# The expert work of a token mixer and router cut into five groups of chunks in place of four

## The chip, the core and the metric

One core of a Trainium2 chip runs the whole kernel. The metric is the device time in microseconds: 777.89 us is the median of three runs of the kernel before (777.68 to 777.95). The five engines are called PE (TensorE, with PEld for its weight loads), DVE (VectorE), ACT (ScalarE), POOL (GpSimd) and SP (SyncE, which issues most DMAs).

## The reference

```
h = tok(x)                  # four shifted copies + layer norm + 8x8 patch convolution: 16 images x 169 tokens x 128
h = concat([h, txt], 1)     # + 512 text tokens per batch item: 16 x 681 tokens, 128 wide
h = h + attn(layernorm(h))  # p_t * cumsum(p_s * x) @ mix_w.T + mix_b, along the tokens
h = h + ffn(layernorm(h))

# ffn: 8 experts, hidden width 256, the best 2 of 8 for each token
logits = xf @ Wg;  topw, topi = top_k(logits, 2);  topw = softmax(topw)
g, u = split(xf @ Wgu[e] + bgu[e]);  eo[e] = (silu(g) * u) @ Wd[e] + bd[e]
out  = sum over the two chosen experts of weight * eo
```

## The kernel before

The tokens are cut into 23 chunks of at most 4 x 128 tokens: 7 image chunks (4 x 104 tokens, the last one half as wide) and 16 text chunks, in the order 3 image, 4 text, 4 image, 12 text. Each chunk goes through attention, the second layer norm, the router (logits, the two best experts), and gets a place for each of its (token, expert) pairs. POOL then writes the chunk's normed rows to those places in the DRAM buffer `xbuf` with indirect DMAs, called scatters here (L1051, 8 for a chunk of width 4).

The chunks are gathered into groups (`GROUPS`, L67). When a group's last chunk has its places, the numbers of tokens of each expert are known and the group is closed: DVE makes a table of expert tiles (`tile_table`) and turns places in `xbuf` into places in `ybuf` (`places_of_results`), SP fills the gaps with zero rows (`pad`, 8 DMAs). From then on the group's expert tiles can run. A tile is 256 rows of one expert: SP loads its rows (L567) and its expert's weights (L570, 450 KB), PE turns the rows (`tile_T`, L791), multiplies by the gate and up weights (`gate_up`), ACT and DVE make silu(g) * u (L947, L1491), PE multiplies by the down weights (`down`), DVE adds the bias (`row_keep`, L1500) and SP stores 256 rows to `ybuf` (L576). After the group's last tile is stored, POOL fetches each token's two result rows with indirect DMAs, called gathers (L1065, 8 for a chunk of width 4); DVE weighs and adds them (`combine`, L1511 and L1515) and SP stores the chunk of the output (L583 for text, L589 for images).

How many tiles a group needs is fixed ahead of the data: `KT[g] = (2 * tokens + 8 * 255) // 256`, since each of 8 experts can leave a tile nearly empty. Likewise `xbuf` has room for the worst case, plus 8 spare tiles of zero rows for each group.

The order of the work on every engine is written by one clock of slots: iteration i has 16 slots, and slot number 16 * i + s says which step is issued. In iteration i chunk i is placed (slot 4) and scattered (slots 5 to 14), while later chunks stand at earlier steps (`AT`). A closed group's tiles begin at slot 6 of the iteration after its last chunk, and `spread` lays them evenly over the slots up to where the next group's tiles begin; the last group has 2 slots per tile. The gathers of a group are spread in the same way, from 6 slots behind its last tile to where the next group's tiles end. Engines wait for each other by semaphores, so a slot has no fixed length; all engines pass the slots in this order, and a late step holds back what is queued behind it on its engine. In the first iterations the second half of the images is worked in as well.

```
TILE_FROM = [b * SLOTS + 6 for a, b in GROUPS]
TILE_TO = TILE_FROM[1:] + [TILE_FROM[-1] + 2 * KT[-1]]
GATHER_FROM = [b + GATHER_LAG for b in TILE_TO]           # 6 slots
GATHER_TO = TILE_TO[1:] + [TILE_TO[-1] + GATHER_LAG + 16]
```

Of the kernel before, what the change touches and what calls it, by code (L numbers as in the profile page):

```python
# [63 lines left out]
SLOT = 256  # L64
SUB = SLOT // P
SHIFT = 8
GROUPS = [(0, 4), (4, 12), (12, 19), (19, 23)]  # L67


def width(n):  # L70
# [7 lines left out]
def cols_of(n):  # L78
    return parts(n) * width(n)


def group_of(n):
    return next(g for g, (a, b) in enumerate(GROUPS) if a <= n < b)


NTOK = [sum(cols_of(n) for n in range(a, b)) for a, b in GROUPS]
CAP = [(-(-n // SLOT) + 1) * SLOT for n in NTOK]
KT = [(2 * n + E * (SLOT - 1)) // SLOT for n in NTOK]
ROW0 = [sum(E * CAP[j] + E * SLOT for j in range(g)) for g in range(len(GROUPS) + 1)]
TILE0 = [sum(KT[:g]) for g in range(len(GROUPS) + 1)]  # L90
TILES = TILE0[-1]
KMAX = max(KT)

QUAD = 4
GROUP_POS = max(b - a for a, b in GROUPS) * W4 * 2


def tile_group(k):
    return next(g for g in range(len(GROUPS)) if k < TILE0[g + 1])

# [1525 lines left out]
```

## Time and profile before

| | |
|---|---|
| median of the runs | 777.89 us |
| the profiled execution | 779.29 us, its span 777.5 us |
| PE matmul busy | 579.0 us (74%) |
| PE weight load busy | 510.3 us (66%) |
| POOL busy | 474.0 us (61%) |
| DVE busy | 463.0 us (60%) |
| ACT busy | 235.7 us (30%) |
| mean granted TensorE clock | 0.815 of full speed |

The share of each engine is a mean over stages that differ. A stage can be found by the placing of a chunk, the DVE instruction of L1366: chunk 0 is placed at 93.56 us, chunk 3 at 147.38, chunk 11 at 307.07, chunk 18 at 472.93 and the last one, chunk 22, at 606.51. PE's last tile ends near 725 us, and the rest is POOL's gathers with DVE and SP behind them.

### The profile page before, as it was taken

To read this page: it belongs to the slowest core of one execution; us is meant where nothing else is said; L and a number is where in the kernel's file an instruction comes from. 1 tells how busy PE (TensorE), PEld (TensorE's weight loads), DVE (VectorE), ACT (ScalarE), POOL (GpSimd) and SP (SyncE) were. 2 spreads that over 40 slices of the span, in tenths; PEclk is the share of its full clock that TensorE was granted. 3 is DMA by queue.
4 is the path that set the end of the run, shared out by engine and by line. 5 is a ranking of instruction groups with operands and counts; after the bars stand their busy time and mean duration, and the time that the engine had idled before them with its cause. 6 is when DMAs were issued, how large, how long until landed. Compare 5 with 4: busy or idle time off the path is not lost. (4 is left out here: it accounts for less than half of the span.)

```text
span 777.5 us, 12251 instructions
## 1 busy us (share of the span) xinstructions
PE 579.0 (74%) x3221; PEld 510.3 (66%) x3221; DVE 463.0 (60%) x1838; ACT 235.7 (30%) x576; POOL 474.0 (61%) x504
## 2 busy tenths in 40 slices
PE   3793558666896986799998988889798788988200
PEld 2692447654775775688787877779687676887100
DVE  4667787765546567747767666736565553565322
ACT  3511412210423233234344441434433232433000
POOL 5513377734757564547776775637777772777674
PEclk9997556765968688769989896979999989999755
DMA  7298000204446353367776665569878787999322
GB/s 151 58 319 204 14 24 26 84 15 165 124 144 169 114 174 107 109 204 225 209 220 200 181 211 179 154 215 274 248 214 248 253 239 222 292 315 296 100 81 61
DMA packets 85130, 132.93 MB, mean 171 GB/s; under 512 B 14818, under 2 KB 58330, under 8 KB 85062
## 3 DMA queue, kind: packets, MB, share of 16 engines
q1 hardware_dynamic: 73062, 109.39, 46.9%
q0 software_dynamic: 11520, 22.35, 9.4%
q10 hardware_dynamic: 480, 0.41, 0.4%
q8 instruction: 27, 0.44, 0.2%
q14 instruction: 41, 0.34, 0.1%
HBM read 92.01 MB, written 43.75 MB: 175 GB/s over the span
## 5 line engine op out<-in xcount | busy, mean ns | idle before, releaser
L619 PE MATMUL gu<-space,wts 128*128 128x256 f32 x912 | 252.8, 419 | 1.8 <-DVE space L1491 1.8
L1051 POOL DMA_INDIRECT xbuf<-x,pos x180 | 185.0, 1028 | 68.5 <-issue 59.2
L1065 POOL DMA_INDIRECT gat<-ybuf,ypos x180 | 176.7, 982 | 72.3 <-issue 56.9
L1491 DVE SCALAR_TENSOR_TENSOR space<-gu,wts,space 128x256 f32<-128x256 f32 x228 | 108.4, 481 | 186.3 <-ACT space L947 113.5
L947 ACT ACTIVATE space<-gu,wts 128x256 f32<-128x256 f32 x228 | 107.2, 472 | 318.3 <-PE gu L619 311.5
L619 PEld LDWEIGHTS gu<-space,wts 128*128 128x128 f32 x912 | 181.2, 213 | 24.5 <-DVE space L1491 2.6
L619 PEld LDWEIGHTS dn<-wts,space 128*128 128x128 f32 x912 | 128.4, 206 | 34.5 <-DVE space L1491 28.2
L619 PE MATMUL dn<-wts,space 128*128 128x128 f32 x912 | 132.4, 292 | 20.8 <-DVE space L1491 20.0
L993 POOL TENSOR_TENSOR rs<-ve,nhalf 128x4 f32<-128x4 f32 (+2 forms) x39 | 41.3, 1058 | 74.0 <-DVE ve L1288 43.3
L791 PE MATMUL xTp<-cst,space 128*128 128x128 f32 x228 | 51.1, 310 | 20.3 <-DMA space<-xbuf 20.2
L1500 DVE TENSOR_TENSOR space<-dn,wts 128x256 f32<-128x256 f32 x114 | 47.3, 415 | 3.8 <-PE dn L619 3.7
L791 PEld LDWEIGHTS xTp<-cst,space 128*128 128x128 f32 x228 | 30.5, 159 | 28.2 <-DMA space<-xbuf 24.0
L941 ACT COPY space<-xTp 128x256 f32<-128x256 f32 x114 | 41.4, 363 | 23.0 <-PE xTp L791 23.0
L619 PE MATMUL mx<-mixT,yT 128*128 128x128 f32 x128 | 34.3, 430 | 14.3 <-DVE rank L1366 8.5
L1511 DVE SCALAR_TENSOR_TENSOR gat<-gat,w,space 128x128 f32<-128x128 f32 x64 | 18.2, 346 | 44.6 <-DMA gat<-ybuf,ypos 44.6
L619 PEld LDWEIGHTS mx<-mixT,yT 128*128 128x128 f32 x128 | 31.1, 327 | 16.2 <-issue 16.1
L619 PEld LDWEIGHTS tr<-wg,x2T 128*128 128x128 f32 (+1 forms) x180 | 32.3, 263 | 4.8 <-issue 2.9
L929 ACT ACTIVATE x<-space,sh,rs 128x128 f32<-128x128 f32 x64 | 26.3, 486 | 25.7 <-POOL sh L1035 25.7
L619 PE MATMUL dn<-wtokT,space 128*104 128x128 f32 x260 | 34.0, 296 | 0.0
L619 PEld LDWEIGHTS dn<-wtokT,space 128*104 128x104 f32 x260 | 33.4, 192 | 0.0
L1041 POOL TENSOR_TENSOR ex<-euler,gap 128x4 f32<-128x4 f32 (+2 forms) x23 | 23.6, 1026 | 12.5 <-DVE gap L1314 12.0
L619 PE MATMUL tr<-wg,x2T 128*128 128x8 f32 (+1 forms) x180 | 30.9, 300 | 0.0
(190 smaller groups left out, 690.2 us busy)
## 6 DMA issues: line engine op xcount, KB each, us to landing
wts<-wall SPq DMA_DIRECT2D x114, 450.0 KB, 4.5
space<-xbuf SPq DMA_DIRECT2D x114, 128.0 KB
ybuf<-space SPq DMA_DIRECT2D x114, 128.0 KB
xt<-in_txt_dram SPq DMA_DIRECT2D x16, 256.0 KB, 4.1
xbuf<-zero_rows SPq DMA_DIRECT2D x4, 1024.0 KB, 11.2
xbuf<-zero_rows SPq DMA_DIRECT2D x32, 128.0 KB
out_dram<-gat SPq DMA_DIRECT2D x16, 256.0 KB
xbuf<-x,pos POOLq DMA_INDIRECT x180
```

The costliest lines, as they stand in the source:

```text
L619: return nc.tensor.matmul(o, l, r, start=a, stop=z_)
L791: last = nc.tensor.transpose(xT_ps[:, s * P:(s + 1) * P], xrow[k % NX][:, s * D:(s + 1) * D], ident)
L929: last = nc.scalar.activation(x2[n % NX2][0:p, j * D:(j + 1) * D], h1_of(n)[0:p, j * D:(j + 1) * D], ACT.Identity, bias=sh2[0:p, j:j + 1], ...
L941: copy(xT[k % 2], xT_ps[:, 0:SLOT]).then_inc(W.xs_ok, 1)
L947: nc.scalar.activation(sil[q % 3], gu_ps[q % 3][:, 0:SLOT], ACT.Silu, bias=wts[k % NW][:, W_B + t:W_B + t + 1]).then_inc(W.sil_ok, 1)
L993: tt(out_[0:p, 0:w], var[0:p, 0:w], nhalf[0:p, 0:w], ALU.pow).then_inc(done, 1)
L1041: tt(ex[0:p, 0:w], euler[0:p, 0:w], gap[0:p, 0:w], ALU.pow).then_inc(W.ex_ok, 1)
L1051: nc.gpsimd.indirect_dma_start(out=xbuf, out_offset=bass.IndirectOffsetOnAxis(pos[0:p, c:c + 1], 0), in_=x2[n % NX2][0:p, m // 2 * D:(m // ...
L1065: nc.gpsimd.indirect_dma_start(out=gat[b][0:p, (k * W4 + j) * D:(k * W4 + j + 1) * D], out_offset=None, in_=ybuf[g], in_offset=bass.Indire ...
L1491: V.scalar_tensor_tensor(hid[q % 4], gu_ps[q % 3][:, SLOT:2 * SLOT], wts[k % NW][:, W_B + HT + t:W_B + HT + t + 1], sil[q % 3], ALU.add, A ...
L1500: V.tensor_tensor(yrow[k % NYB].rearrange("p (s d) -> p s d", s=SUB), dn_ps[k % 2][:, 0:SUB * D].rearrange("p (s d) -> p s d", s=SUB), wts ...
L1511: last = V.scalar_tensor_tensor(rows[1][j], rows[1][j], wn[1][j], h1_of(n)[0:p, j * D:(j + 1) * D], ALU.mult, ALU.add)
```

## The change

`GROUPS` has five groups that end at chunks 4, 10, 16, 20 and 23, in place of four that end at 4, 12, 19 and 23. Nothing else is edited; everything that hangs on the table follows.

```diff
-GROUPS = [(0, 4), (4, 12), (12, 19), (19, 23)]
+GROUPS = [(0, 4), (4, 10), (10, 16), (16, 20), (20, 23)]
```

What follows from it, by the kernel's own formulas:

| | before | after |
|---|---|---|
| tokens of each group | 1760, 3504, 3584, 2048 | 1760, 2784, 2768, 2048, 1536 |
| tiles of each group | 21, 35, 35, 23 (114) | 21, 29, 29, 23, 19 (121) |
| slots where the tiles begin | 70, 198, 310, 374 | 70, 166, 262, 326, 374 |
| slot where the last tiles end | 420 | 412 |
| gathers of each group | 32, 60, 56, 32 (180) | 32, 48, 44, 32, 24 (180) |
| slots of the gathers | 204 to 310, 316 to 374, 380 to 420, 426 to 442 | 172 to 262, 268 to 326, 332 to 374, 380 to 412, 418 to 434 |
| pad DMAs, spare DMAs of 1 MB | 32, 4 | 40, 5 |

PE's queue around the place of chunk 10, kernel before (mx<-mask are the ranks of a chunk, mx<-mixT the attention's product of a later one, gu and dn are tile work, x22 a buffer of normed rows):

```order
L744 MATMUL tr<-cst,x22 128x128 x4
L619 MATMUL mx<-mask,tri_r 104x16
L619 MATMUL mx<-mask,ones_r 104x8
L619 MATMUL mx<-seen0,ones_r 104x16
L619 MATMUL gu1<-space,wts0 128x256 x2
L619 MATMUL dn0<-wts4,space 128x128 x4
L619 MATMUL mx<-mixT,yT 128x128 x4
L619 MATMUL mx<-mixb2,ones_r 128x512
L619 MATMUL tr<-wg,x2T 128x8 x4
L791 MATMUL xTp<-cst,space 128x128 x2
L619 MATMUL gu2<-space,wts1 128x256 x2
```

The same place in the changed kernel:

```order
L744 MATMUL tr<-cst,x22 128x128 x4
L619 MATMUL gu2<-space,wts0 128x256 x2
L619 MATMUL dn1<-wts4,space 128x128 x4
L619 MATMUL dn0<-wts0,space 128x128 x4
L619 MATMUL mx<-mask,tri_r 104x16
L619 MATMUL mx<-mask,ones_r 104x8
L619 MATMUL mx<-mixT,yT 128x128 x4
L619 MATMUL mx<-mixb2,ones_r 128x512
L791 MATMUL xTp<-cst,space 128x128 x4
L619 MATMUL gu0<-space,wts1 128x256 x2
```

Chunk 10 now begins a group: its ranks no longer add what was counted before (the seen row is gone). The first group's tiles end here with two down products in a row, and the next group's begin with two turned tiles in a row; before, tile work ran across this place without a seam.

POOL's queue at its very end, kernel before (xbuf<- are scatters, gat<- gathers, ybuf1 to ybuf3 the result buffers of groups 1 to 3, counted from 0):

```order
L1051 DMA xbuf<-x21,pos 104448x128
L1065 DMA gat<-ybuf1,ypos 104x128
L1051 DMA xbuf<-x21,pos 104448x128
L1065 DMA gat<-ybuf1,ypos 128x128 x8
L1065 DMA gat<-ybuf2,ypos 128x128 x56
L1065 DMA gat<-ybuf3,ypos 128x128 x32
```

And in the changed kernel:

```order
L1051 DMA xbuf<-x21,pos 108544x128
L1065 DMA gat<-ybuf2,ypos 128x128
L1051 DMA xbuf<-x21,pos 108544x128
L1065 DMA gat<-ybuf2,ypos 128x128 x8
L1065 DMA gat<-ybuf3,ypos 128x128 x32
L1065 DMA gat<-ybuf4,ypos 128x128 x24
```

Behind the last scatter stand 8 + 32 + 24 gathers in place of 8 + 56 + 32, and the final block, which waits for the last tile, has 24 in place of 32.

## Rows read from the trace of the kernel before

**Rows 1.** The page: busy time of two engines, share of the span, instructions.

```profile
PE 579.0 (74%) x3221; PEld 510.3 (66%) x3221; DVE 463.0 (60%) x1838; ACT 235.7 (30%) x576; POOL 474.0 (61%) x504
```

**Rows 2.** Chain that ended last, from 722 us: start, us, what.

```profile
725.30 2.62 DMA ybuf<-space
...
729.46 0.95 POOL gat L1065
...
767.14 0.95 POOL gat L1065
```

**Rows 3.** Timeline of POOL: start, us, what, idle before and its releaser.

```profile
655.46 1.07 POOL L1065 DMA_INDIRECT gat<-ybuf,ypos  x1 [14.52 <-DMA ybuf<-space]
...
725.53 0.95 POOL L1065 DMA_INDIRECT gat<-ybuf,ypos  x1 [0.30 <-issue]
```

**Rows 4.** Stretches: length, PE, PEld, DVE, ACT, POOL busy (instructions), clock, DMA share, GB/s.

```profile
201.10:251.00 49.90, 38.90 (x221) 33.50 (x219) 26.28 (x144) 16.66 (x43) 32.44 (x36) 0.83 0.55 159
251.00:307.10 56.10, 45.32 (x223) 38.60 (x223) 34.56 (x160) 19.06 (x49) 30.34 (x36) 0.77 0.46 135
307.10:331.40 24.30, 17.99 (x83) 15.73 (x83) 17.85 (x80) 6.06 (x15) 11.63 (x13) 0.71 0.32 101
331.40:355.90 24.50, 23.09 (x114) 19.63 (x114) 13.93 (x61) 9.64 (x25) 14.03 (x16) 0.76 0.67 217
355.90:472.90 117.00, 108.31 (x601) 95.10 (x601) 79.35 (x340) 46.45 (x120) 84.76 (x90) 0.91 0.70 207
472.90:501.50 28.60, 24.95 (x125) 21.82 (x125) 19.74 (x84) 9.07 (x23) 17.37 (x18) 0.82 0.53 162
501.50:539.30 37.80, 33.93 (x185) 30.43 (x185) 19.41 (x72) 13.22 (x33) 19.51 (x21) 0.86 0.73 227
539.30:606.50 67.20, 59.14 (x353) 53.31 (x352) 37.67 (x144) 22.57 (x57) 51.15 (x53) 0.95 0.81 244
...
645.00:728.10 83.10, 70.18 (x419) 61.88 (x418) 44.53 (x126) 27.91 (x69) 53.80 (x56) 0.98 0.86 272
```

**Rows 5.** Stretches, tile turns of L791 alone, two for a tile: length, PE, PEld, clock.

```profile
251.00:307.10 56.10, 3.70 (x16) 2.32 (x16) 0.77 0.46 135
...
355.90:472.90 117.00, 10.87 (x50) 6.38 (x50) 0.91 0.70 207
...
539.30:606.50 67.20, 7.22 (x36) 4.57 (x36) 0.95 0.81 244
```

**Rows 6.** The page's costliest groups, PE matmuls of the tiles, 114 tiles.

```profile
L619 PE MATMUL gu<-space,wts 128*128 128x256 f32 x912 | 252.8, 419 | 1.8 <-DVE space L1491 1.8
...
L619 PE MATMUL dn<-wts,space 128*128 128x128 f32 x912 | 132.4, 292 | 20.8 <-DVE space L1491 20.0
...
L791 PE MATMUL xTp<-cst,space 128*128 128x128 f32 x228 | 51.1, 310 | 20.3 <-DMA space<-xbuf 20.2
```

**Rows 7.** Timeline of PE around 505 us, the first tiles of the third group.

```profile
505.16 0.44 PE L791 MATMUL xTp<-cst,space 128*128 128x128 f32 x2 [0.82 <-DMA space<-xbuf]
508.33 0.69 PE L791 MATMUL xTp<-cst,space 128*128 128x128 f32 x2 [2.73 <-DMA space<-xbuf]
```

**Rows 8.** Timeline of DVE, placing of chunks 16 and 17.

```profile
424.24 0.19 DVE L1366 TENSOR_TENSOR rank<-mx,off_f 128x32 f32<-128x32 f32 x1
...
448.60 0.18 DVE L1366 TENSOR_TENSOR rank<-mx,off_f 128x32 f32<-128x32 f32 x1
```

**Rows 9.** Chain that ended last, 660 to 700 us.

```profile
668.53 1.73 PE gu L619 x8
...
674.21 1.74 PE gu L619 x8
...
694.77 0.43 SPq L583
...
695.38 4.95 DMA space<-xbuf
```

**Rows 10.** Timeline of PE, a wait for a tile's rows in the last group.

```profile
700.37 0.44 PE L791 MATMUL xTp<-cst,space 128*128 128x128 f32 x2 [1.20 <-DMA space<-xbuf]
```

## The prediction

> **What bounds the kernel now.** I read the chain that ended last first, then POOL's timeline, then a table of stretches cut at the placing of chunks. The chain ends in one engine: after the last tile's results have landed (725.30 + 2.62 = 727.9 us) POOL issues 32 gathers, one each (767.14 - 729.46) / 30 = 1.256 us, and nothing overlaps them [rows 2]. The stretch before, 645.0 to 728.1 us, holds the 23 tiles of the last group. PE is busy for 70.2 of 83.1 us at clock 0.98, and POOL gathers there without a break from 655.46 to 726.5 us [rows 3, 4]: PE and POOL end within 2 us of each other, so both bound it.
>
> Farther back the reader is to see three densities [rows 4, 5]. From 251.0 to 307.1 us three chunks pass with 16 tile turns, which is 8 tiles: 18.7 us a chunk at 2.67 tiles, PE busy 81%, clock 0.77. From 355.9 to 472.9 us five chunks pass with 25 tiles: 23.4 us a chunk at 5, PE busy 93%, clock 0.91. From 539.3 to 606.5 us two chunks pass with 18 tiles: 33.6 us a chunk at 9, PE busy 88%, while POOL issues 53 instructions in 67.2 us, 1.27 us each, which is its full pace. So the kernel is near PE's limit from 331 us on, near POOL's as well from about 520 us, and has room only before 331 us. Over the whole span PE is busy 74% and POOL 61% [rows 1], which hides this.
>
> **The change part by part.** The work is moved as the table of slots shows: 7 more tiles in all, 4 fewer behind slot 374, hence 11 more before it.
>
> *Gathers behind the last tile.* 24 in place of 32: 8 x 1.256 = 10.0 us less [rows 2]. Nothing hides it; the combine and the store behind it stay. This is the surest term: **-10.0**.
>
> *The last group's tiles.* 19 in place of 23. Where nothing disturbs it a tile takes (674.21 - 668.53) / 2 = 2.84 us [rows 9], so four are 11.4 us. The stretch has also PE waits, as of 1.20 us at 700.37 us, for a tile's rows, whose load stood in SP's queue behind an output store [rows 9, 10]; SP is in order, and the store waits for DVE's combine, that for POOL's gathers. Before, 7 chunks were stored in this stretch, now 4, and POOL has 32 x 1.256 = 40 us of gathers beside some 60 us of tiles, so it no longer bounds. I take three such waits, 1.3 us each with the slower start behind them, as gone: **-15.4**. Bounds: -11.4 without them; -20 if PE ran all 19 tiles at 2.84 (54 us, beside 4.4 us from 645.0 to the first tile's product and some 4.5 us of filling and draining, 63 in place of 83).
>
> *Slots 70 to 198.* Before, 21 tiles; now 21 and 29 x 32/96 = 9.67, so +9.67 tiles in eight chunks' time, 3.8 a chunk on the mean. From 18.7 us at 2.67 tiles to 23.4 us at 5 is 4.7 / 2.33 = 2.0 us for one more tile [rows 4, 5]; it covers what is hidden in waits and what the higher clock gives back. 9.67 x 2.0 = **+19.3**. Bounds: 0, since PE is idle for 28.1 us from 201.1 to 331.4 us (130.3 less 102.2 [rows 4]) and 9.67 x 2.84 = 27.5 us would just fit; +37 where nothing is hidden and the clock stays at its mean, by the busy time of a tile, (252.8 + 132.4 + 51.1) / 114 = 3.83 us [rows 6]. PE's waits there are for other engines in the middle of a chunk's chain (attention, norm, router), and a tile placed in front of a chain step delays that step, so I stay at the measured slope between the two.
>
> *Slots 198 to 262.* 19.3 tiles in place of 20, at 2.55 us (next term): **-1.7**.
>
> *Slots 262 to 374.* 52 tiles in place of 15 + 35 = 50. One more tile costs (33.6 - 23.4) / 4 = 2.55 us between 5 and 9 a chunk [rows 4, 5], so PE's side says +5.1. POOL's side: slot 268 lies halfway between the placings of chunks 16 and 17, at 436.4 us [rows 8], and slot 374 at 645, so the slots 268 to 374 last 208.6 us. POOL had 72 gathers, 48 scatters and 22 small instructions there, 142 x 1.27 = 180 us; it now has 92 gathers, 162 x 1.27 = 206 us. It fits, but with 3 us of slack where there were 28, and the norm's scale (POOL, L993 and L1035) that each chunk needs is queued behind those gathers. Two engines that are both nearly full and wait for each other in every chunk lose something: I add 2 us. **+7**. Bounds: +3 (a tile hidden for the most part, since the densities are more even now, 7.3 and 7.7 a chunk in place of 5 and then 8.75), +15 (each of the six chunks waits 2 us for POOL).
>
> *One more closing and one more seam.* Closing a group lengthens its chunk: 24.3 against 18.7 us for chunk 11 and 28.6 against 23.4 us for chunk 18, so 5.4 us: the table and the changed places on DVE, and PE's next product behind them. The seam, where the tiles of one group drain and the first rows of the next are loaded, costs 24.5 - 23.4 = 1.1 us at chunk 12 and 37.8 - 33.6 = 4.2 us at chunk 19 [rows 4], where PE stands for 0.82 and 2.73 us waiting for rows [rows 7]; mean 2.7. There are three of each between the first and the last group where there were two. The new tables are smaller (29 tiles in place of 35), so of 8.1 us I take **+7**; bounds +4 (partly under POOL's queue in the full stretch) and +10. The 8 more pad DMAs are in it. The spare DMA of 1 MB stands long before the first tile, beside the image stage, in which no tile is loaded: 0, and up to +1 if it delays a load.
>
> Sum: -10.0 - 15.4 + 19.3 - 1.7 + 7 + 7 = +6.2 us. The profiled execution took 779.3 us (its span 777.5), which makes 785.5; the runs' median is 1.4 us under it, so 784.1 us by the median.
>
> **The rivals.**
>
> *A, the early tiles are nearly free (faster).* The place is slots 70 to 198. The clock is 0.83 and 0.77 from 201.1 to 307.1 us and 0.91 where 5 tiles a chunk run [rows 4]. If the added tiles both fill PE's waits and lift the clock, the 84.2 us that PE is busy there would shrink by 84.2 x (1 - 0.80 / 0.91) = 10 us, and that offsets half of 19.3. The term is then between 0 and 9 and the sum between -13 and -4: 765 to 774 us, middle 770. It decides from 1.4 us a tile downwards, where the sum is below zero. For it: PE idles for 28 us there, and the three chunks from 201.1 to 251.0 us take only 16.6 us each with tiles among them. Against it: the measured slope holds the clock's gain already, and the waits are in the chain of the chunk. By the Trainium skill, "TensorE: Matmul & The Clock Gate", section on the HAM clock gate, the array's default state is throttled and activity releases it, which is the rule that speaks for this rival; by that rule the trace agrees in direction, clock 0.77 at 2.67 tiles a chunk against 0.91 at 5.
>
> *B, it cancels.* The early tiles cost 1.4 us each (13.5 us) and the rest stands: the sum is +0.4, 778 us. For it stands only that it lies between A and the forecast.
>
> *C, POOL takes over (clearly slower).* In slots 268 to 374 POOL becomes the bound of each chunk: 15 in place of 7, and early tiles cost 2.84 us each (27.5): the sum is +22, 800 us. For it: 16.8 gathers a chunk with 8 scatters stand in POOL's queue for chunks 20 to 22, and 13 for chunks 17 to 19 where there were about 5. Against it: POOL gets through 53 instructions in two chunks already now.
>
> *D, the move isn't made.* The queues show it is: 24 gathers behind the last tile's result. No chance of its own.
>
> **How the numbers follow.** A run of this kernel can be told from no change by about 0.2%, 1.6 us. The forecast, sums of +2 to +16, has 0.48, and its own range is 780 to 794 us. A has 0.27, B 0.12, C 0.13. Nearly all of the forecast and C is slower: 0.48 + 0.13, 0.61 with a little of B to either side. A is faster, 0.27. That leaves 0.12 within 0.2%. All terms at their low ends would make -24, all at their high ends +40, but they are unlike in cause and will not fall together; the range that leaves 2 in 10 outside runs from just under A's middle to C's lower half: 769 to 797 us.
>
> **What would show it.** (1) The gathers behind the last landing: 24 at 1.256 us, 30 us in place of 40. (2) From the first load of the last group to that landing: about 68 us in place of 83, with POOL idle for 15 us or more before the final block. (3) The three chunks from the placing of chunk 5 to that of chunk 8, where nothing but the number of tiles has changed (48 slots at 0.219 tiles in place of 0.164, so 2.6 more), last 55 us in place of 49.9 [rows 4]; under 52, A holds. (4) From chunk 16's placing to the last group's first load: 221 us before, now about 232, with POOL's instructions at 1.3 us apart nearly throughout; 240 or more would be C. (5) A closing near chunk 9 and chunk 15, each some 5 us longer than its neighbours. The prediction is wrong if the time is below 777 us, and its reason is wrong if the early part is not longer although the time is.

## The result, and the profile after

The changed kernel takes 814.17 us (median of four runs, 812.26 to 815.42) against 777.78 us, which is the kernel before with a fourth run: a ratio of 1.0485, 95% interval 1.0447 to 1.0523. It is 36 us slower where 6 us were forecast, and outside the range of 769 to 797 us. The sign was right, the size was not. The profiled execution took 815.4 us, its span 813.6 us.

I split the span at the placing of the last chunk. Before it the kernel lost 61.3 us (606.5 to 667.8 us), where the sum had 31.6; behind it 25.2 us were gained (171.0 to 145.8 us), where it had 25.4. So the tail is as forecast and all of the error lies in front of it. Cut at the placings of the chunks 4, 12, 16 and 22, the front reads 151.7, 92.9 and 182.3 us before and 169.7, 108.9 and 211.1 us after: +18.0, +16.0 and +28.8 us (chunk 4 itself is placed 1.5 us earlier).

The chain that ended last, from 768 us (start, us, what), answers to [rows 2]: 24 gathers, (801.90 - 774.40) / 22 = 1.250 us each.

```profile
771.67 1.88 DMA ybuf<-space
...
774.40 0.94 POOL gat L1065
...
801.90 0.94 POOL gat L1065
...
803.15 2.48 DMA gat<-ybuf,ypos
```

POOL's timeline (start, us, what, idle before) answers to [rows 3]. It now stands still for 28 us until the last tile is stored, so it no longer bounds the last group.

```profile
745.27 0.95 POOL L1065 DMA_INDIRECT gat<-ybuf,ypos  x1 [0.30 <-issue]
774.40 0.94 POOL L1065 DMA_INDIRECT gat<-ybuf,ypos  x1 [28.18 <-DMA ybuf<-space]
```

The stretches of the changed kernel (length, then busy time of PE, PEld, DVE, ACT, POOL, clock, DMA share, GB/s), cut at the placings of the same chunks as [rows 4]; the last row runs from the last group's first load to the landing of its last tile.

```profile
202.80:252.30 49.50, 44.98 (x270) 39.89 (x270) 28.97 (x151) 19.34 (x50) 31.82 (x36) 0.90 0.67 194
252.30:320.40 68.10, 57.55 (x294) 49.52 (x294) 43.87 (x193) 23.37 (x61) 35.74 (x39) 0.80 0.56 171
320.40:347.90 27.50, 19.70 (x120) 17.62 (x120) 16.31 (x72) 9.27 (x24) 17.39 (x18) 0.95 0.60 180
347.90:370.90 23.00, 20.45 (x108) 17.55 (x108) 14.46 (x64) 9.08 (x23) 16.72 (x19) 0.83 0.69 198
370.90:522.80 151.90, 128.21 (x672) 111.57 (x672) 92.72 (x390) 51.84 (x132) 97.35 (x104) 0.83 0.63 191
522.80:552.90 30.10, 28.72 (x168) 26.00 (x168) 18.20 (x75) 12.41 (x31) 22.72 (x24) 0.89 0.78 243
552.90:598.60 45.70, 31.88 (x165) 27.37 (x163) 25.36 (x101) 10.21 (x26) 27.41 (x29) 0.81 0.50 154
598.60:667.80 69.20, 54.84 (x300) 47.78 (x301) 32.86 (x132) 20.40 (x51) 43.56 (x45) 0.86 0.70 220
...
705.00:773.60 68.60, 58.77 (x342) 51.45 (x342) 34.37 (x97) 23.08 (x57) 30.50 (x32) 0.95 0.78 247
```

The first row is the surprise for the early tiles: 49.5 us with 270 matmuls where there were 49.9 us with 221, at clock 0.90 in place of 0.83. The fifth row holds most of the loss: the chunks 13 to 17 take 151.9 us in place of 117.0, with PE busy 84% and not 93%, and at clock 0.83 and not 0.91. POOL's 104 instructions there would fit in 132 us at 1.27 us each, so POOL doesn't bound it.

The clearest case is the chunks 13 and 14, which hold no closing and no seam and the same tile work to within a few matmuls. Kernel before and changed kernel:

```profile
355.95:376.20 20.25, 19.69 (x120) 17.57 (x120) 14.61 (x64) 9.27 (x24) 14.74 (x17) 1.00 0.76 224
376.20:398.16 21.96, 20.11 (x120) 17.49 (x120) 16.70 (x72) 9.27 (x24) 17.20 (x19) 1.00 0.76 222
```

```profile
370.91:400.45 29.54, 25.48 (x120) 21.55 (x120) 16.48 (x72) 9.45 (x24) 18.66 (x20) 0.76 0.56 168
400.45:427.40 26.95, 21.85 (x117) 19.59 (x118) 15.96 (x70) 8.63 (x22) 17.03 (x18) 0.82 0.53 163
```

They take 56.5 us in place of 42.2. Over the whole profiled execution PE is busy for 601.9 us in place of 579.0 (3347 matmuls, 126 more) and idle for 211.7 us in place of 198.5, although 10 us of idle time behind the last tile are gone. The 22.9 us of busy time are no more than seven tiles at 3.83 us [rows 6], 26.8 us; the other 23 us are idle time in front of the last tile.

What the engines wait for (us in total, times, longest), from the first tiles to the last group's first load. Kernel before, 185 to 645 us:

```profile
PE xTp L791 <- DMA space<-xbuf: 12.2, 6, 3.4
DVE gat L1511 <- DMA gat<-ybuf,ypos: 11.9, 6, 4.5
PE mx L619 <- DVE rank L1366: 8.3, 10, 1.8
...
PE mx L619 <- DVE need_i L1389: 5.8, 2, 3.6
```

Changed kernel, 185 to 705 us:

```profile
DVE gat L1511 <- DMA gat<-ybuf,ypos: 31.9, 8, 6.1
PE xTp L791 <- DMA space<-xbuf: 25.8, 16, 4.6
PE mx L619 <- DVE rank L1366: 25.1, 12, 7.3
...
PE mx L619 <- DVE need_i L1389: 14.4, 3, 8.7
```

Three waits have grown: DVE in `combine` for gathers that have not landed (+20 us), PE's attention product (`mix`, mx) for DVE's placing or table (+25 us), and PE for the rows of a tile (+14 us). Against them stands PE's wait for the mask of the routing (L1328), which fell from 8.2 to 1.0 us. Neither of the first two was a term of the forecast. One of them in full, the timelines of DVE and of PE around the placing of chunk 12 in the changed kernel:

```profile
344.12 1.14 DVE L1511 SCALAR_TENSOR_TENSOR gat<-gat,w,h_img 104x128 f32<-104x128 f32 x4 [5.08 <-DMA gat<-ybuf,ypos]
...
347.85 0.18 DVE L1366 TENSOR_TENSOR rank<-mx,off_f 128x32 f32<-128x32 f32 x1
```

```profile
339.80 1.05 PE L619 MATMUL dn<-wts,space 128*128 128x128 f32 x8
348.18 1.04 PE L619 MATMUL mx<-mixT,yT 128*128 128x128 f32 x3 [7.33 <-DVE rank L1366]
```

The combine of chunk 0 stands in slot 2 of iteration 12, and the placing of chunk 12 in slot 4 behind it. DVE waits 5.1 us for the gathers to land, spends 2.2 us on the combine, and PE, which may not overwrite the ranks before they are read, waits 7.33 us. By the slot formulas the changed kernel puts combines into slots 2, 1, 4, 1 and 1 of the iterations 12, 18, 19, 21 and 22; the kernel before has them in slots 4 and below only in iterations 16 and 22. The one in slot 4 stands behind the placing but ahead of the table in slot 5. (Iterations from 23 on place no chunk.)

### The profile page after: what moved, and what is told of

Read it like the earlier page. It is cut to its first block, busy times and chain, and to the rows that moved or that the text cites. A ratio compares the mean times of both kernels' runs of the same rounds, so it can differ in the third digit from the quotient of the medians.

```text
span 813.6 us, 12721 instructions
## 1 busy us (share of the span) xinstructions
PE 601.9 (74%) x3347; PEld 529.6 (65%) x3347; DVE 470.3 (58%) x1880; ACT 244.1 (30%) x597; POOL 475.5 (58%) x506
## 4 chain that ended last, share of the span: by engine, by line
PE 18%; POOL 11%; DMA 6%; issue 6%; DVE 6%; SPq 2%; ACT 1%; POOLq 0%; DVEq 0%; ACTq 0%
PE gu L619 9%; POOL gat L1065 7%; PE dn L619 5%; POOL xbuf L1051 3%; DMA space<-xbuf 3%; DMA gat<-ybuf,ypos 3%; PE mx L619 2%; PE xTp L791 2%; DVE space L1491 1%; DVE gat L1511 1%; PE tr L619 1%; DVE gat L1515 1%; POOL rs L993 1%; SPq L542 1%; DVE space L1500 1%
## 5 line engine op out<-in xcount | busy, mean ns | idle before, releaser
L619 PE MATMUL gu<-space,wts 128*128 128x256 f32 x968 | 272.0, 423 | 4.1 <-DVE space L1491 3.8
L1491 DVE SCALAR_TENSOR_TENSOR space<-gu,wts,space 128x256 f32<-128x256 f32 x242 | 115.1, 479 | 207.0 <-ACT space L947 147.9
L947 ACT ACTIVATE space<-gu,wts 128x256 f32<-128x256 f32 x242 | 114.0, 472 | 357.2 <-PE gu L619 349.6
L619 PEld LDWEIGHTS gu<-space,wts 128*128 128x128 f32 x968 | 193.3, 214 | 31.1 <-DVE space L1491 5.0
L619 PEld LDWEIGHTS dn<-wts,space 128*128 128x128 f32 x968 | 135.6, 205 | 33.9 <-DVE space L1491 27.2
L619 PE MATMUL dn<-wts,space 128*128 128x128 f32 x968 | 139.1, 290 | 19.4 <-DVE space L1491 19.2
L791 PE MATMUL xTp<-cst,space 128*128 128x128 f32 x242 | 55.0, 313 | 34.0 <-DMA space<-xbuf 33.4
L619 PE MATMUL mx<-mixT,yT 128*128 128x128 f32 x128 | 34.4, 434 | 39.6 <-DVE rank L1366 25.2
L791 PEld LDWEIGHTS xTp<-cst,space 128*128 128x128 f32 x242 | 32.8, 161 | 42.6 <-DMA space<-xbuf 39.4
L619 PEld LDWEIGHTS mx<-mixT,yT 128*128 128x128 f32 x128 | 31.1, 327 | 42.9 <-issue 42.9
L941 ACT COPY space<-xTp 128x256 f32<-128x256 f32 x121 | 44.0, 363 | 36.4 <-PE xTp L791 36.4
L1500 DVE TENSOR_TENSOR space<-dn,wts 128x256 f32<-128x256 f32 x121 | 50.2, 415 | 4.6 <-PE dn L619 4.6
L905 ACT ACTIVATE z_i<-h_img,ish,irs 104x128 f32<-104x128 f32 x26 | 10.9, 483 | 53.7 <-POOL ish L1012 52.6
```

The source lines that it names most:

```text
L619: return nc.tensor.matmul(o, l, r, start=a, stop=z_)
L791: last = nc.tensor.transpose(xT_ps[:, s * P:(s + 1) * P], xrow[k % NX][:, s * D:(s + 1) * D], ident)
L905: last = nc.scalar.activation(z_i[0:PI, i * D:(i + 1) * D], h_tiles[:, nx0 + i, g, :], ACT.Identity, bias=ish[0:PI, i:i + 1], scale=irs[0: ...
L941: copy(xT[k % 2], xT_ps[:, 0:SLOT]).then_inc(W.xs_ok, 1)
L947: nc.scalar.activation(sil[q % 3], gu_ps[q % 3][:, 0:SLOT], ACT.Silu, bias=wts[k % NW][:, W_B + t:W_B + t + 1]).then_inc(W.sil_ok, 1)
L1491: V.scalar_tensor_tensor(hid[q % 4], gu_ps[q % 3][:, SLOT:2 * SLOT], wts[k % NW][:, W_B + HT + t:W_B + HT + t + 1], sil[q % 3], ALU.add, A ...
```

## The experiments

I write "the changed one" for the kernel with five groups and "the four groups" for the kernel before, and give each run's median beside its ratio to the kernel before on the same chip. The ratios have intervals of some 0.5 to 1% to either side, so 4 to 8 us. The runs were made in batches on different chips, on which the kernel before takes 777.6 to 781.7 us by the median; where two runs of different batches are compared, the difference of their ratios is given too.

**Combines later.** Theory 1 is that the combine's lag of 3 slots behind the last gather is too short; rival 2 is that the tiles and closings simply cost more than I priced.

```diff
-SUM_LAG = 3
+SUM_LAG = 8
```

> The changed kernel with the combine of each chunk (and its store behind it) placed 8 slots behind its last gather in place of 3. Theory 1: DVE stands in combines whose gathers have not landed (31.9 us before the last group's end, against 14.7 us in the kernel before), and as it is in order, placing, hidden and down products wait behind it; then this gives back 15 to 25 us, 790 to 799 us. Rival 2: the time is the price of 7 tiles, the closings and the lower clock, and the combine's wait only shows slack that is there anyway: within 3 us of 814.

Measured 785.57 us, ratio 1.0077 (1.0031 to 1.0124): 29 us faster than the changed kernel. The listing of DVE's combine waits has none left before the tail. By the ratios the gain is 32 us. Theory 1 holds and gave more than expected; rival 2 is out as the only cause.

> The kernel before with the same 8 slots in place of 3. Theory 1: its combines wait 14.7 us, and few of these stretches end in a PE wait, so 3 to 8 us faster, 770 to 775 us. Rival 2: no change, 778 us.

Measured 764.38 us, ratio 0.9809 (0.9738 to 0.9880). The four groups gain 14 us by the same edit, more than I expected. These two runs share a chip and stand 21 us apart, where the kernels as they are stand 36 us apart. So about half of what the lag costs was there before the change, and some 15 us of it came with the change.

**The price of a tile.**

```diff
+MORE = [10, 0, 0, 0]          # the other run: [0, 0, 10, 0]
+SPARE = E + max(MORE)
-KT = [(2 * n + E * (SLOT - 1)) // SLOT for n in NTOK]
+KT = [(2 * n + E * (SLOT - 1)) // SLOT + m for n, m in zip(NTOK, MORE)]
-ROW0 = [sum(E * CAP[j] + E * SLOT for j in range(g)) for g in range(len(GROUPS) + 1)]
+ROW0 = [sum(E * CAP[j] + SPARE * SLOT for j in range(g)) for g in range(len(GROUPS) + 1)]
```

> The kernel before with 10 more tiles in the first group (31 in slots 70 to 198; the tiles added are rows of zeros that no result is taken from). Prices a tile in the sparse stretch by itself. My prediction's slope: +20 us (798). Its rival A, nearly free: under +9 us. Theory 1 says the price is low, +0 to +10, since slots 70 to 148 of the changed kernel took 4 more tiles at +0.7 us.

Measured 790.13 us, ratio 1.0122 (1.0046 to 1.0199): about 12 us for ten tiles, 1.2 us each; the interval of the ratio makes it 0.4 to 1.5, and not the 2.0 of the forecast. The same three chunks as in the first of [rows 4], from the placing of chunk 5 to that of chunk 8, lie at 208.62 to 257.10 us in that kernel and show why:

```profile
208.62:257.10 48.48, 42.85 (x282) 37.98 (x282) 30.47 (x156) 20.86 (x54) 31.77 (x35) 1.00 0.72 214
```

They take 48.5 us in place of 49.9 although PE has 282 matmuls in place of 221. It is busy for 42.9 in place of 38.9 us and its clock is full where it was 0.83: the work that was there runs faster, and the rest of the new work fills waits.

> The kernel before with 10 more tiles in the third group (45 in slots 310 to 374). Prices a tile in the dense stretch. The prediction's slope: +25 us (803). If POOL bounds that stretch: under +15. If PE does at full clock: +28.

Measured 808.24 us, ratio 1.0362 (1.0284 to 1.0439): by the ratio 28 us or 2.8 us a tile, with an interval of 2.2 to 3.4, so it isn't told apart from the forecast's 2.55. POOL doesn't bound that stretch, or it would have been under 15 us.

**Tile steps out of the placing's slot.** With later combines the changed kernel still waits in another way. PE's timeline at the same step, `mix` behind the placing of chunk 14, in the changed kernel with later combines:

```profile
393.52 2.21 PE L619 MATMUL mx<-mixT,yT 128*128 128x128 f32 x8 [1.66 <-DVE rank L1366]
```

and in the kernel before:

```profile
376.53 1.64 PE L619 MATMUL mx<-mixT,yT 128*128 128x128 f32 x6 [0.44 <-DVE rank L1366]
```

In slot 4 DVE does its part of a tile step first, which waits for PE and ACT, and then the placing. When the step in slot 4 is a tile's second half, PE has a down product to do meanwhile and waits 0.44 us; when it is a first half, it has none and waits 1.66 us. With 35 tiles over 112 slots there are exactly ten steps in each iteration and slot 4 holds a second half at seven placings in a row (chunks 13 to 19), and the clock is 1.00 over the first two of them. (It isn't at the next three: 0.87, 0.79 and 0.93 over the chunks 15, 16 and 17.) With 29 tiles over 96 slots the pattern drifts: slot 4 holds a first half at the chunks 13, 14, 18 and 19. The edit:

```diff
+def phased(at):
+    if at >= TILE_TO[-2] or at in TILE_FROM:
+        return at
+    if at % SLOTS == 4:
+        return at + 1
+    if at % SLOTS == 6 and at - 1 not in TAKEN and at - 2 not in TAKEN:
+        return at - 1
+    return at
...
+UNITS_AT = by_slot([(phased(at), item) for at, item in UNIT_PAIRS])
```

(`UNIT_PAIRS` is the list that `UNITS_AT` was made of, `TAKEN` its slots. The moved step then stands behind the placing on DVE, and ahead of `mix` on PE.)

> The changed kernel with combines 8 slots behind, and in it the tile step that falls on slot 4 of an iteration moved to slot 5 (and from 6 to 5 where 4 and 5 have none). In slot 4 DVE puts its half of a tile step ahead of the placing for which PE's next mix in slot 5 waits; the spread of 29 tiles puts a tile's first half there, and PE then waits 1.66 us and runs at a lower clock behind it, where 35 tiles over 112 slots put a second half there in each chunk (0.44 us, clock 1.00). Theory 3, this phase is what keeps the changed kernel slow after the combines are moved: 8 to 16 us faster than 785.6, 770 to 778. Rival 2, the price of tiles and closings alone: within 3 us of 785.6.

Measured 758.93 us, ratio 0.9679 (0.9611 to 0.9747): 27 us faster than with later combines alone (31 by the ratios), more than any theory had. PE's waits for the placing, from the first tiles to the last chunk, in the changed kernel with later combines:

```profile
PE mx L619 <- DVE rank L1366: 13.3, 11, 2.0
...
PE mx L619 <- DVE need_i L1389: 9.0, 3, 4.0
```

and with the steps moved as well:

```profile
PE mx L633 <- DVE need_i L1403: 7.0, 3, 4.0
...
PE mx L633 <- DVE rank L1380: 1.6, 2, 1.4
```

So 12 us of waits for the placing have gone. Over the whole execution PE's idle time fell by 9 us (from 190.0 to 181.4), since other waits grew, and its busy time by 16 us (from 594.6 to 578.3) for the same 3347 matmuls: the larger part of the gain is work done at a higher clock. Two stretches show it: the same chunks 12 to 14 of the changed kernel with later combines

```profile
342.60:367.30 24.70, 19.68 (x110) 17.04 (x108) 16.64 (x73) 9.12 (x23) 19.46 (x21) 0.93 0.75 215
367.30:393.20 25.90, 22.10 (x120) 19.12 (x120) 16.66 (x73) 9.45 (x24) 18.84 (x20) 0.87 0.57 171
393.20:417.10 23.90, 23.30 (x117) 20.53 (x118) 13.78 (x62) 8.64 (x22) 16.01 (x18) 0.79 0.66 203
```

and with the steps moved

```profile
333.70:356.40 22.70, 17.59 (x108) 15.44 (x107) 15.78 (x70) 8.16 (x21) 17.72 (x19) 1.00 0.74 212
356.40:379.40 23.00, 19.91 (x123) 17.44 (x122) 16.70 (x72) 9.37 (x24) 17.92 (x20) 1.00 0.70 206
379.40:402.20 22.80, 19.00 (x119) 16.73 (x118) 14.49 (x64) 9.37 (x24) 18.00 (x20) 1.00 0.73 218
```

The clock stays at its full level, and about the same number of matmuls takes 19.0 us where it took 23.3.

What lets the clock fall isn't shown. With later combines alone it falls to its lower level within 2 us of the wait of 1.66 us at 393.52 (first row). But in the kernel before it does so within 3 us of a wait of 0.44 us at 398.49 (second row), and with the steps moved it stays full through a wait of 2.80 us (third row):

```profile
395.50:404.50 9.00, 9.00 (x30) 7.55 (x30) 1.97 (x7) 1.05 (x3) 5.39 (x7) 0.50 0.52 184
401.50:407.00 5.50, 5.50 (x20) 4.78 (x20) 1.41 (x3) 0.94 (x3) 3.86 (x6) 0.50 0.32 77
395.95 1.16 PE L633 MATMUL dn<-wts,space 128*128 128x128 f32 x8 [2.80 <-DVE space L1505]
```

The edit also does a second thing. By the kernels' formulas the last tile step of a group stood in slot 4 together with the first loads of the next, and behind the move its stores stand behind those loads on SP: so at three of the four seams of the changed kernel and at one of the three of the four groups.

> The kernel before with combines 8 slots behind and the same move of tile steps. Theory 3: its waits there are short already (0.44 us in five chunks), so 0 to 6 us faster than 764.4. Rival: slower by a few us, as tile steps then lie closer together in slot 5.

Measured 750.34 us, ratio 0.9569 (0.9493 to 0.9646), 14 us faster than with later combines alone (19 by the ratios). I had expected 0 to 6. Here the placing isn't the main gain: the chunk at the seam, 19, went from 38.8 to 31.2 us. SP's queue shows the stores of the last tiles behind the next group's first loads there (490.46 and 487.07 us), where they stood ahead of them (490.24 and 494.47 us). The edit bundles two causes; the runs with early loads below tell them apart in part.

**Each edit alone.**

```diff
-SUM_LAG = 8
+SUM_LAG = 3
```

> The changed kernel with combines 3 slots behind as at first, and only the tile steps of slot 4 moved to slot 5 (6 to 5 where 4 and 5 have none). If the two causes add up: 814.2 - 26.6 = 788. If the move works only where combines don't block: near 805.

Measured 784.97 us, ratio 1.0133 (1.0046 to 1.0220).

> The kernel before with only the tile steps of slot 4 moved. If the causes add up: 778 - 14 = 764; otherwise nearer to 775.

Measured 759.65 us, ratio 0.9795 (0.9709 to 0.9881). In the changed kernel the two edits add up (29 + 29, together 55 us), in the four groups nearly (14 + 18, together 27), within what the intervals allow. So neither edit works through the other.

**A closing and a seam at equal tiles.** The second group is split into chunks 4 to 7 and 8 to 11 with 43 tiles in slots 198 to 310, and stands beside a kernel with one group and 43 tiles there (`MORE = [0, 8, 0, 0]`).

```diff
-GROUPS = [(0, 4), (4, 12), (12, 19), (19, 23)]
+GROUPS = [(0, 4), (4, 8), (8, 12), (12, 19), (19, 23)]
-TILE_FROM = [b * SLOTS + 6 for a, b in GROUPS]
+TILE_FROM = [70, 198, 258, 310, 374]
...
+GATHER_FROM = [204, 316, 346, 380, 426]
+GATHER_TO = [310, 346, 374, 420, 442]
```

> The kernel before with combines 8 slots behind and 8 more tiles in its second group (43 in slots 198 to 310; the tiles added are rows of zeros that no result is taken from). At 2 to 3 us a tile: 780 to 788. It stands beside the run with the second group split in two, which has as many tiles there.

Measured 785.02 us, ratio 1.0030 (0.9994 to 1.0065), so against the 764.4 us of another chip 8 tiles cost 20.6 us here, 2.6 each; by the ratios it is 17 us, 2.1 each.

> The kernel before with combines 8 slots behind and its second group (chunks 4 to 11) split into chunks 4 to 7 and 8 to 11: one more closing, one more seam, 23 and 20 tiles over the same slots 198 to 310 and the same slots for gathers. Less the run with 8 more tiles it prices one closing and seam at equal tiles: the prediction's term 7 us; the intervals of the last traces (closing 7 to 8, seam 5) say 10 to 14.

Measured 795.67 us, ratio 1.0171 (1.0112 to 1.0229): 10.7 us for one closing and one seam (same chip), where the forecast had 7 for one of each. Chunk by chunk the closing (chunk 7) shows 2 us and the chunk with the seam (15) 11 us, so it is the seam. This closing stands in the sparse stretch, though: in the dense one, the closing's chunk 18 lasts 28.9 us with later combines beside 22.3 for chunk 17, and still 26.6 beside 22.0 with all three edits. PE's timeline at the seam of the split group:

```profile
433.33 1.16 PE L619 MATMUL dn<-wts,space 128*128 128x128 f32 x8 [2.00 <-DVE space L1491]
439.00 0.69 PE L791 MATMUL xTp<-cst,space 128*128 128x128 f32 x2 [4.51 <-DMA space<-xbuf]
441.60 0.69 PE L791 MATMUL xTp<-cst,space 128*128 128x128 f32 x2 [1.90 <-DMA space<-xbuf]
```

The seam stands at slot 258, with nothing beside it but the turns of a chunk (L744), which PE gets to behind the two waits for rows; the seams of the changed kernel stand at slot 6 of an iteration, where `mix` and `logits` can fill a part. I take the price as an upper end for them; no run shows that.

**First loads ahead of the last stores.** A seam is long where SP, in order, has to wait for the rows of the last tiles before it issues the next group's first load. By the formulas the stores stand first at all four seams of the changed kernel, and at two of the three of the four groups, not at the last one: the change made two more such seams.

```diff
-OPENS_AT = by_slot([(TILE_FROM[g] - 2, g) for g in range(len(GROUPS))])
+OPENS_AT = by_slot([(TILE_FROM[g] - 5, g) for g in range(len(GROUPS))])
```

> The changed kernel with combines 8 slots behind, no tile step moved, but the loads of a group's first three tiles issued on SP 5 slots ahead of its first tile in place of 2, so that they stand ahead of the stores of the last tiles of the group before. Theory 4, a seam is long because SP is in order and the first load waits behind stores whose rows aren't made: 3 to 5 us for each of the seams at chunks 10, 16 and 20, so 9 to 15 us faster than 785.6. Theory 3 alone (the placing in slot 4 holds the time): no change.

Measured 773.95 us, ratio 0.9960 (0.9914 to 1.0005): 12 us faster than 785.6 (9 by the ratios), as theory 4 says.

> The kernel before with combines 8 slots behind and the first loads 5 slots ahead. Theory 4: the seams at chunks 12 and 19, 5 to 10 us faster than 764.4. In the kernel with moved tile steps the seam at chunk 19 lost 7.6 us (38.8 to 31.2), since its last stores then stood behind the loads: this run tells which part of the 14 us was the seam. Theory 3 alone: no change.

Measured 753.41 us, ratio 0.9682 (0.9597 to 0.9766): 11 us faster than 764.4 (10 by the ratios), a little above the 5 to 10 expected. PE's timeline at the seam of chunk 19, with the loads 2 slots ahead

```profile
496.59 0.44 PE L791 MATMUL xTp<-cst,space 128*128 128x128 f32 x2 [0.81 <-DMA space<-xbuf]
499.89 0.69 PE L791 MATMUL xTp<-cst,space 128*128 128x128 f32 x2 [2.86 <-DMA space<-xbuf]
500.37 3.62 PE L619 MATMUL gu<-space,wts 128*128 128x256 f32 x8
```

and 5 slots ahead:

```profile
500.39 0.44 PE L791 MATMUL xTp<-cst,space 128*128 128x128 f32 x2
501.38 0.41 PE L791 MATMUL xTp<-cst,space 128*128 128x128 f32 x2 [0.55 <-ACT space L941]
501.62 1.89 PE L619 MATMUL gu<-space,wts 128*128 128x256 f32 x8
```

The wait of 2.86 us goes, and the eight products behind it take 1.89 us and not 3.62, at the upper level of the clock (granted 1.00) and not the lower (0.50). This seam costs twice.

**All three edits.**

> The changed kernel with all three edits: combines 8 slots behind, tile steps off slot 4, first loads 5 slots ahead. If seam and placing are separate costs: 758.9 - 11.6 = 747. If the moved steps had taken the seam's gain already: 757 to 759.

Measured 760.04 us, ratio 0.9768 (0.9706 to 0.9830), no faster than without the early loads; its runs spread from 753.9 to 763.7. Beside the run with early loads and unmoved steps (773.95 us) it shows what the moved steps give where SP's loads stand first in any case: 14 us, 15 by the ratios.

> The kernel before with all three edits. Its moved steps took the seam at chunk 19 already (7.6 us), so of the 11 us only 3 to 4 are left: 746 to 748. The changed kernel then stands 0 to 3 us from it.

Measured 743.71 us, ratio 0.9529 (0.9473 to 0.9584): the fastest kernel of the study, 4.7% faster than the kernel before and 8.7% faster than the changed one. The expectation that the changed one would come within 3 us of it failed: it stands 16 us from it. Here the moved steps give 10 us beside the run with early loads (753.41), 12 by the ratios.

A last run asked whether the short last group can be had without a fifth group:

```diff
-GROUPS = [(0, 4), (4, 12), (12, 19), (19, 23)]
+GROUPS = [(0, 4), (4, 13), (13, 20), (20, 23)]
```

> All three edits with four groups that end at 4, 13, 20 and 23: 114 tiles, 19 in the last group, 24 gathers behind it, but 35 tiles and 68 gathers beside the chunks 20 to 22. Tail: -25 us. Front: POOL has 26 gathers and 8 scatters a chunk, 43 us a chunk at 1.27 us each in place of 30, about +30. So 745 to 760, and slower than the four groups of before if POOL bounds it.

Measured 749.44 us, ratio 0.9612 (0.9559 to 0.9666). The short last group gives back less than the dense stretch before it takes: the chunks 20 and 21 last 40.4 and 38.0 us, between the 33 us that 11.7 tiles make at 2.84 us and the 43 us of POOL's full pace.

The pairs side by side, each pair on one chip; the last column counts the seams at which the last stores stand ahead of the first loads, by the formulas:

| | five groups | four groups | difference | such seams |
|---|---|---|---|---|
| as they are | 814.2 | 777.8 | 36 | 4 and 2 |
| combines later | 785.6 | 764.4 | 21 | 4 and 2 |
| combines later, early loads | 774.0 | 753.4 | 21 | 0 and 0 |
| tile steps moved | 785.0 | 759.7 | 25 | 1 and 1 |
| combines later, steps moved | 758.9 | 750.3 | 9 | 1 and 1 |
| all three | 760.0 | 743.7 | 16 | 0 and 0 |

The last two differences are not told apart, by the intervals of their ratios (1.1 and 2.4%, each within about 1%); nor is the last one from the 21 us above it.

## Why the prediction was wrong

*Gathers behind the last tile, -10.0.* Right: 30 us in place of 40.

*The last group, -15.4.* Right: 68.6 us from the first load to the landing, 68 forecast, 83.1 before [rows 4], so 14.5 less; POOL idle for 28 us where 15 or more were said. Of the three waits inside the group that were to go two went; one of 1.71 us is left (748.60 us).

*Slots 70 to 198, +19.3.* Wrong, too high. The three chunks from the placing of chunk 5 took 49.5 us, where the forecast's own test was 55 and "under 52, A holds". Rival A was right of this place: added tiles filled waits and lifted the clock, at 1.2 us a tile by the run that added ten. What failed here is the slope of 2.0 us, taken between chunks at 2.67 tiles and chunks at 5; the measured price in the sparse stretch is 1.2. That from the placing of chunk 4 to that of chunk 12 the kernel still lost 18.0 us, near the 19.3, is luck: this stretch also holds a closing, a seam and the combine of chunk 0, which waits 5.1 us ahead of the placing of chunk 12.

*Slots 198 to 262, -1.7.* Wrong, and by the most beside its size: from the placing of chunk 12 to that of chunk 16 it was 108.9 us in place of 92.9, +16.0, with one closing among them. The chunks 13 and 14 alone make +14.3 with equal tile work. They take 49.8 us with later combines and 45.8 with moved steps as well, so 10.7 of the 14.3 us hang on where combines and tile steps stand.

*Slots 262 to 374, +7.* Size wrong. From the placing of chunk 16 to the last group's first load the forecast had 232 us; it took 248 (456.7 to 705.2). By the forecast's own test, 240 or more, this would be rival C, but it isn't POOL: its 171 instructions there would fit in 217 us at 1.27 us each. The stretch holds three of the long waits of PE: 6.22 us at chunk 18, 8.74 us at chunk 19 and 5.95 us in a down product at chunk 22, each behind a combine that waited for its gathers. The price of a tile there, 2.8 us measured, isn't what failed: on two tiles it makes half a microsecond.

*One closing and seam, +7.* Wrong in its parts more than in its sum: 10.7 us at equal tiles in the run that split a group, nearly all of it in the seam, where I had put 5.4 on the closing and 2.7 on the seam. For a closing in the dense stretch the four groups show 5 to 7 us, so 5.4 may hold there. And I took the seams as alike: at the last one of the kernel before the first loads stand ahead of the last stores, and in the changed kernel they don't.

*What the sum had no term for.* This is the failed step: I took it that moving tiles and gathers to other slots leaves the waits between steps as they were, and priced numbers of things alone. The prediction does say that a tile placed in front of a chain step delays that step, but it left this inside the slope. The place of a step in its iteration has a price of its own. Combines that fell just ahead of the placing or the table cost 15 us of the 36: the difference between the kernels falls from 36 to 21 when combines come later, and DVE's waits for gathers are gone. Tile steps in front of the placing cost the changed kernel another 14 us and seams with the stores first 12 us, but the four groups pay 10 and 11 us for the same. Of the difference between the kernels the moved steps take 4 us (from 21 to 16, loads early in both) to 12 us (from 21 to 9, where the order at the seams moved with them); the intervals don't tell these two apart, nor the smaller one from nothing. What is left, 9 to 16 us, is of the size of the sum, +6.2. That its terms were right one by one isn't shown: the early tiles cost less and the seam more, and they make up for each other.

That a wait was to be had could be seen. The kernel before has DVE waits of 4.47 and 2.52 us in combines, in the trace where the chain of waits passes through a gather's landing, and the order of both kernels tells which combine stands ahead of which placing.

What stays open: the 27 us that the moved steps give the changed kernel are not split exactly. With SP's loads early in both runs the moved steps give 14 us, which is the placing and its clock; the other 13 us would be three seams, for which early loads at four seams gave 12. These runs come from three chips. Open too is why the clock holds in some chunks and falls in others, and what the last 9 to 16 us between the kernels consist of.

## What to carry to other kernels

In a schedule written by slots a change of counts also shifts the phase of every step against the others: before pricing the work that moves, list which step now stands directly in front of the one that another engine waits for. An in-order engine should do the work of its critical chain before any step that may wait for a DMA; here moving one step by one slot and another by five took 55 us off the five groups and 27 us off the four, while no other grouping tried beat the one with groups ending at 4, 12 and 19. Where an engine's clock follows its activity, a bubble can be paid for twice, and work added to a sparse stretch costs less than its busy time.

## What the runs showed of the hardware

A TensorE that is kept busier does the same work faster by more than I had counted: with ten tiles added to the first group, the three chunks behind the placing of chunk 5 went from a granted clock of 0.83 to 1.00 and held 282 matmuls in place of 221 in 48.5 us in place of 49.9. At the seam of chunk 19 the eight products behind a wait of 2.86 us took 3.62 us at a granted clock of 0.50, and 1.89 us at 1.00 without the wait. "TensorE: Matmul & The Clock Gate" of the Trainium skill, in its section on the HAM clock gate, says that activity releases the throttle; the traces agree, with these numbers. The length of one wait doesn't foretell the clock here: it stayed at 1.00 through a wait of 2.80 us and fell to 0.50 behind one of 0.44 us.

A gather of 128 rows takes some 5 us from the start of its issue until DVE may read it in the dense stretches, against some 2.5 us with nothing beside it: of the landings on the chain of the changed kernel, two took 5.30 us (553.21) and 5.41 us (582.38), and the last one of all 2.48 us.
